# First layer: softmax denominators from blocks summed by GpSimd, once a chunk, and numerators in 32-column tiles

## What is computed

```python
kc = k.reshape(B, H, Nc, CHUNK, Dh)          # Nc = 8 chunks of 256 keys
scores = einsum('bhnd,bhjcd->bhnjc', q, kc) / sqrt(Dh)
scores = clip(scores, -10, 10)
scores = where(mask == 0, -10, scores)       # mask: adjacency
attn = softmax(scores, axis=-1)              # over the 256 keys of a chunk
ctx = einsum('bhnjc,bhjcd->bhnd', attn, vc)  # summed over the chunks
out = layernorm(ctx @ Wo.T + bo + x) * gamma + beta
```

## Time and profile before

| | |
|---|---|
| median of 3 runs | 4966.05 us (4965.57 to 4966.41) |
| the profiled execution | 4965.84 us, span 4964.0 us |
| TensorE (PE) busy | 4617.1 us, 93% |
| VectorE (DVE) busy | 3681.5 us, 74% |
| ScalarE (ACT) busy | 2924.1 us, 59% |
| GpSimd (POOL) busy | 1947.7 us, 39% |

### The profile page before, as it was taken

The page is one execution under the profiler, slowest core; times in us unless marked ns, Lnnn a source line. Parts: engine busy times, 40 slices in busy tenths (PEclk is TensorE's granted clock), DMA queues, the critical chain, the costliest instruction groups (busy, mean ns, idle before and its releaser), DMA issues. The chain is left out here.

```text
span 4964.0 us, 78134 instructions
## 1 busy us (share of the span) xinstructions
PE 4617.1 (93%) x31752; PEld 2705.9 (55%) x31752; DVE 3681.5 (74%) x5434; ACT 2924.1 (59%) x3373; POOL 1947.7 (39%) x1391
## 2 busy tenths in 40 slices
PE   5999999998999999999999899947999999999998
PEld 2334333333433433433333343327999999999998
DVE  4676677678577677667767857747889889898896
ACT  3553555455455355355445545518878888788785
POOL 1133222232232223223223323225657576666585
PEclk9999999999999999999999999968999999999999
DMA  5000000000100000000000000011112112111111
GB/s 186 1 18 9 26 9 18 26 9 9 34 9 9 19 16 18 9 26 14 13 26 9 13 14 9 9 35 49 50 47 77 30 68 76 34 65 54 47 56 44
DMA packets 126665, 160.50 MB, mean 32 GB/s; under 512 B 8545, under 2 KB 108897, under 8 KB 126305
## 3 DMA queue, kind: packets, MB, share of 16 engines
q1 hardware_dynamic: 126304, 155.49, 9.7%
HBM read 121.64 MB, written 33.83 MB: 31 GB/s over the span
## 5 line engine op out<-in xcount | busy, mean ns | idle before, releaser
L421 ACT ACTIVATE e_sb<-e_sb 128x1024 f32<-128x1024 f32 x1024 | 1080.4, 1056 | 1186.6 <-DVE e_sb L512 1171.4
L512 DVE SCALAR_TENSOR_TENSOR e_sb<-psS,mask 128x1024 f32<-128x1024 f32 x1024 | 1225.8, 1216 | 473.8 <-PE psS L628 460.1
L1229 PE MATMUL psA<-xy,ring_p 128*128 128x195 bf16 x8192 | 1399.4, 248 | 19.6 <-DVE red L1109 19.6
L1229 PE MATMUL psA<-xy,ring_s 128*128 128x195 bf16 x8192 | 1399.0, 248 | 0.0
L628 PE MATMUL psS<-qT,kT 64*128 64x512 f32 x4096 | 1089.7, 617 | 57.3 <-DVE e_sb L512 57.3
L1029 ACT ACTIVATE ring_s<-eiB,ejb 128x1024 int8<-128x1024 f32 x1024 | 1088.5, 1135 | 8.5 <-PE psA L1229 8.5
L641 PE MATMUL psN<-e_sb,v_sb 128*64 128x512 f32 x4096 | 1000.1, 609 | 0.0
L352 POOL TENSOR_TENSOR ctxT<-ctxT,num 128x512 f32<-128x512 f32 x384 | 486.3, 1275 | 1009.0 <-DVE num L492 1009.0
L1229 PEld LDWEIGHTS psA<-xy,ring_p 128*128 128x128 fp8e4 x8192 | 799.5, 98 | 24.9 <-DVE red L1109 22.5
L1229 PEld LDWEIGHTS psA<-xy,ring_s 128*128 128x128 fp8e4 x8192 | 798.7, 97 | 8.0 <-issue 0.3
L628 PEld LDWEIGHTS psS<-qT,kT 64*128 64x128 f32 x4096 | 460.2, 187 | 464.2 <-issue 234.7
(11 more groups left out here) (104 smaller groups left out, 4010.5 us busy)
## 6 DMA issues: line engine op xcount, KB each, us to landing
eiB<-ei_between SPq DMA_DIRECT2D x64, 512.0 KB, 4.2
xin<-x SPq DMA_DIRECT2D x32, 512.0 KB, 6.7
xr<-x SPq DMA_DIRECT2D x32, 512.0 KB, 3.8
x_between<-hy SPq DMA_DIRECT2D x32, 512.0 KB, 2.9
xin<-x_between SPq DMA_DIRECT2D x32, 512.0 KB, 5.6
xo<-x_between SPq DMA_DIRECT2D x32, 512.0 KB, 4.4
out<-o_sb SPq DMA_DIRECT2D x32, 512.0 KB, 5.2
e_sb<-adjT SPq DMA_DIRECT2D x4, 2048.0 KB, 9.6
```

Source lines behind the costliest of these rows:

```text
L421: act.activation(e_sb[:, s % ES], e_sb[:, s % ES], ACT.Exp, scale=SCALE).then_inc(exp_done, 1)
L512: dve.scalar_tensor_tensor(out=e_sb[:, s % ES], in0=psS[:, s % 2], scalar=-CLIP_RAW, in1=mask[:, kb, cols][:, None, :].to_broadcast([P, 2, ...
L1229: ins = pe.matmul(psA[:, i % BANKS, br * PARTS * XW:(br + 1) * PARTS * XW], part[:, n % RING, k, tt * TW + j * P:tt * TW + (j + 1) * P], x ...
```

## The change

GpSimd adds the two exponential blocks of a chunk and pair of heads into a ring of four buffers `e_sum`, at the step after the second block. TensorE takes the denominators from these, four matmuls a chunk instead of eight, four steps after the last block (`DLAG`). The numerators are written as four matmuls with 32 output columns each in place of two with 64. The ring `e_sb` has 8 buffers in place of 6, and VectorE's clip waits for the numerators and the sum of the block it overwrites instead of the denominators. The copy of the sums, the reciprocals and the split move to `ss` 3, (4, 5, 6, 6) and 7, the copy behind the exponential of its step.

```diff
 LAG = 2
-ES = 6
+DLAG = 4
+ES = 8
+SUMS = 4
-SUMS_AT, INV_AT, SPLIT_AT, PICK_AT, RES_AT = 2, 2, 6, 8, 8
+SUMS_AT, INV_AT, SPLIT_AT, PICK_AT, RES_AT = 3, (4, 5, 6, 6), 7, 8, 8
...
+            def sum_blocks(b, g):
+                n = b * (BSTEPS // KPC) + g
+                pool.wait_ge(exp_done, b * BSTEPS + KPC * (g + 1))
+                if n >= SUMS:
+                    pool.wait_ge(sums_done, (n - SUMS) // PAIRS + 1)
+                pool.tensor_tensor(e_sum[:, g % SUMS], e_sb[:, KPC * g % ES], e_sb[:, (KPC * g + 1) % ES], ALU.add)\
+                    .then_inc(esum_done, 1)
...
             def step(b, s):
+                if s % KPC == 0 and KPC <= s <= BSTEPS:
+                    sum_blocks(b, s // KPC - 1)
...
                     if s >= ES:
-                        dve.wait_ge(sums_done, b * (BSTEPS // 2) + chunk_sums_until(s - ES))
+                        dve.wait_ge(num_done, b * GROUPS + (s - ES) // KPC + 1)
+                        dve.wait_ge(esum_done, b * GROUPS + (s - ES) // KPC + 1)
...
-                if half is not None and INV_AT <= ss < INV_AT + TB:
-                    cols = slice((ss - INV_AT) * P, (ss - INV_AT + 1) * P)
-                    if ss == INV_AT:
-                        dve.wait_ge(sums_read, b * HALVES + half + 1)
-                    ins = dve.reciprocal(r_f[:, cols], r_f[:, cols])
+                for j in range(TB):
+                    if half is not None and ss == INV_AT[j]:
+                        cols = slice(j * P, (j + 1) * P)
+                        if j == 0:
+                            dve.wait_ge(sums_read, b * HALVES + half + 1)
+                        ins = dve.reciprocal(r_f[:, cols], r_f[:, cols])
...
-                for i in range(2):
-                    hd = 2 * pair + i
-                    ins = pe.matmul(psN[64 * i:64 * i + 64, pair, :], v_sb[:, kb, hd * D:(hd + 1) * D],
+                for part in range(4):
+                    i, col = part // 2, (2 * pair) * D + 32 * part
+                    ins = pe.matmul(psN[32 * part:32 * part + 32, pair, :], v_sb[:, kb, col:col + 32],
                                     e_sb[:, u % ES, i, :], start=u % KPC == 0, stop=u % KPC == KPC - 1,
...
             def denominators(b, u):
-                if not 0 <= u < BSTEPS or place(u)[1] != PAIRS - 1:
+                if not 0 <= u < BSTEPS or u % SPC != SPC - 1:
                     return
...
+                pe.wait_ge(esum_done, b * GROUPS + PAIRS * (ch + 1))
                 for hd in range(H):
-                    slot = (u - KPC * (PAIRS - 1 - hd // 2)) % ES
                     ins = pe.matmul(psD[32 * hd:32 * hd + 32, :], hot[:, c, :],
-                                    e_sb[:, slot, hd % 2, :], start=first, stop=last,
+                                    e_sum[:, (PAIRS * ch + hd // 2) % SUMS, hd % 2, :], start=c == 0, stop=c == CPH - 1,
```

More of the change, by code:

```diff
@@ L136, in layer0 @@
         e_sb = sb("e_sb", [P, ES, 2, TW])
+        e_sum = sb("e_sum", [P, SUMS, 2, TW])
         num = sb("num", [P, NS, TW])
@@ L177, in layer0 @@
         numcopy_done = sem("numcopy_done")
+        esum_done = sem("esum_done")
         sums_done = sem("sums_done")
@@ L371, in _ @@
                 for s in range(BSTEPS + (GAP if b + 1 < nb else TAIL)):
-                    if s >= HALF:
-                        step(b, s)
+                    step(b, s)
                     if b and s < TAIL - GAP:
@@ L404, in step @@
                     if g >= NS:
-                        act.wait_ge(ctx_done, b * SUMS + sums_until((g - NS) // GPH, (g - NS) % GPH))
+                        act.wait_ge(ctx_done, b * CTX + sums_until((g - NS) // GPH, (g - NS) % GPH))
                     act.activation(num[:, g % NS, :], psN[:, g % PAIRS, :], ACT.Copy).then_inc(numcopy_done, 1)
[L407 to L412, removed]
                 if half is not None and ss == SPLIT_AT:
@@ L421, in step @@
                     act.activation(e_sb[:, s % ES], e_sb[:, s % ES], ACT.Exp, scale=SCALE).then_inc(exp_done, 1)
+                if half is not None and ss == SUMS_AT:
+                    act.wait_ge(sums_done, b * (T * CH) + (half + 1) * CPH)
+                    if half >= 1:
+                        act.wait_ge(r_done, b * HALVES + half)
+                    act.activation(r_f[:, :], psD[:, :], ACT.Copy).then_inc(sums_read, 1)
                 if half is not None and half % 2 == 1 and ss == RES_AT:
@@ L647, in denominators @@
             def denominators(b, u):
[L648 removed]
+                if not 0 <= u < BSTEPS or u % SPC != SPC - 1:
                     return
[L650 to L653 removed]
+                ch = u // SPC
+                c = ch % CPH
+                if c == 0 and ch >= CPH:
+                    pe.wait_ge(sums_read, b * HALVES + ch // CPH)
+                pe.wait_ge(esum_done, b * GROUPS + PAIRS * (ch + 1))
                 for hd in range(H):
[L655 removed]
                     ins = pe.matmul(psD[32 * hd:32 * hd + 32, :], hot[:, c, :],
[L657 removed]
+                                    e_sum[:, (PAIRS * ch + hd // 2) % SUMS, hd % 2, :], start=c == 0, stop=c == CPH - 1,
                                     skip_group_check=True)
@@ L693, in step @@
                 if s > BSTEPS:
+                    denominators(b, s + 1 - DLAG)
                     project(b, s)
@@ L706, in step @@
                     broadcast(b, s + 1)
-                for of in (numerators, denominators):
-                    of(b, s - LAG)
-                    of(b, s + 1 - LAG)
+                numerators(b, s - LAG)
+                numerators(b, s + 1 - LAG)
+                denominators(b, s + 1 - DLAG)
             pe.wait_ge(ident_done, 1)
```

16 lines of the change are left out of this document (5 added, 11 removed).

## The result

The changed kernel takes 5088.26 us (median of four runs, 5082.6 to 5105.39) against 4965.81 us (4964.29 to 4966.41) of the kernel before on the same chip: ratio 1.0252, 95% interval 1.0233 to 1.0271. It is slower by 122 us. The forecast was 62 us slower, and its own case's range ended at 5055. The wide range reached to 5110, but for a rival, longer additions, that did not come about: that it holds the result is luck. The sign and the main mechanisms were right, the size was off by a factor of two.

A forecast was written before the change was run, and what follows sets the result against it. TensorE was taken to bound about half of each layer 0 batch, waiting for VectorE elsewhere. Stretch terms summed to +8.2, taken as +7.7 us a batch, 62 us in eight: 5028 us; own range 4990 to 5055, wide range 4850 to 5110.

The forecast's parts named there:

- longer additions: Rival: GpSimd is the bound, sums longer than 2.36 us or VectorE held twice in a row; 5108 us, chance 0.13.
- opening 16 steps: First 16 steps of a batch: 3 x 0.93 us saved less 1.0 of holds, -1.8 us.
- odd stretch: 16 steps finishing a tile's second half: -3.7 us from fewer denominators, +2.1 from the later split, -1.6 us.
- even with tail: 16 steps finishing a tile's first half, with layer norm: -3.7 + 2.8 + 1.0 + 1.2 + 2.4 = +3.7 us.
- last steps: Last 32 steps of a batch: -4, then the tail's waits and +2.7 for the next batch's layer-norm parts, +4.8 us.
- gap: After a batch's last steps: -0.9 us saved, 2 us lost waiting for GpSimd's queue, +1.1 us.
- What is removed: Denominators: four instead of eight matmuls save 0.93 us a chunk, 238 us at most; numerators in 32-column tiles: 0 us.
- What is moved: Later reciprocals and split: TensorE waits 1.4 us at step 8 (2.1 lost an odd stretch), 2.8 in even ones with layer norm.
- The shared access: GpSimd additions hold VectorE's two-input operations: +2.4 us per tile on the `hy` group, +1.2 on one `tmp` operation.
- the third queue: Gap: TensorE waits for the last sum behind GpSimd's in-order queue, about 2 us; the other two waits 1.5 us each.
- GpSimd that keeps up: Rival: GpSimd keeps up and holds nothing, -14.3 us a batch, 4852 us; chance 0.20.
- the cut in full: Rival: the halved denominators pay fully, 4966 - 238 = 4728 us; chance 0.05.

The follow-up runs named there:

- experiment 4: Changed kernel with each GpSimd sum cut to 64 of 512 columns, so denominators are wrong in value: 4855.2 us, ratio 0.978.
- experiment 1: Kernel before with only the numerators changed, to four tiles of 32 columns: 4930.7 us, ratio 0.9927.
- Experiment 3: Kernel before with 8 exponential buffers and all 512 GpSimd additions, unread, denominators still eight matmuls a chunk: 5134.55 us, ratio 1.0342.
- Experiment 5: Changed kernel with three unread matmuls ahead of TensorE's waits for the split (even stretches with tail) and last sums (gap): 5062.14 us, ratio 1.0194.
- experiment 2: Kernel before with only the sums' copy, reciprocals and split moved to steps 3, (4, 5, 6, 6) and 7: 5128.57 us, ratio 1.0327.
- experiment 9: Changed kernel with reciprocals at steps 4, 4, 5, 5 and the split at 6: 5105.62 us, ratio 1.0281.
- experiment 8: Kernel before with 8 exponential buffers and a 128x2048 GpSimd memset in place of each unread addition: 5038.21 us, ratio 1.0145.

## Why the forecast came out as it did

By its own terms, per batch, against the mean of batches 2 to 7 (the stretch lengths of before and after in brackets). The last two columns take out what the long additions do: the holds and queue waits in the forecast's sum, and the changed kernel less experiment 4, whose additions are short.

| term | forecast | measured | holds and queue waits, forecast | changed kernel less experiment 4 |
|---|---|---|---|---|
| opening 16 steps | -1.8 | -0.5 (36.8, 36.3) | 1.0 | 2.6 |
| first even stretch | -1.6 | -2.1 (39.1, 37.0) | 0 | 0 |
| odd stretch | -1.6 | -2.1 (39.1, 37.0) | 0 | 0 |
| even with tail, stretch 3 | +3.7 | +6.2 (46.5, 52.7) | 4.6 | 6.4 |
| odd, stretch 4 | -0.1 | -1.9 (39.1, 37.3) | 1.5 | 0.3 |
| even with tail, stretch 5 | +3.7 | +4.4 (46.5, 50.8) | 4.6 | 4.5 |
| last steps | +4.8 | +7.3 (94.5, 101.8) | 8.8 | 11.5 |
| gap | +1.1 | +5.5 (59.8, 65.3) | 2 | 5.4 |
| batch | +8.2, taken as +7.7 | +16.8 (401.3, 418.1) | 22.5 | 30.7 |

The holds and waits were put at 22.5 us a batch and cost 30.7, low clock behind them included: 8.2 a batch, 66 us in eight, which is about the 60 that the forecast is short.

**What is removed.** 2048 records of denominators, 0.97 us to the next group against the forecast's 0.93: right. The numerators' 0 was wrong with its sign (experiment 1, -34 us). That the forecast was too low in spite of this gift makes the losses that it missed larger than the difference of 60 us says.

**What is moved.** The odd stretch's wait came out as worked; that the stretch is 0.5 us shorter than forecast is the numerators' shape, 0.6 us there by experiment 1 (39.1 to 38.5). Its timeline, steps 6 to 8:

```profile
1524.13 1.99 PE L640 MATMUL psS<-qT,kT 64*128 64x512 f32 x8
...
1526.64 1.75 DVE L535 RECIPROCAL r_f<-r_f 128x128 f32<-128x128 f32 x2
1527.79 1.04 PE L669 MATMUL psD<-e_sum,hot 128*32 128x512 f32 x8
...
1529.39 0.74 DVE L541 SCALAR_TENSOR_TENSOR r_s<-r_s,lo_rows,r_f 128x512 fp32r<-128x512 f32 x1
1530.19 0.50 PE L686 MATMUL psM<-r_s,pick 64*128 64x512 f32 x1 [1.36 <-DVE r_s L541]
```

The broadcast starts 6.06 us after the scores of step 6 (forecast 6.1) and TensorE waits 1.36 (forecast 1.4). In the even stretch the statistics stand between, and the wait is 3.35 us:

```profile
1483.65 0.74 DVE L541 SCALAR_TENSOR_TENSOR r_s<-r_s,lo_rows,r_f 128x512 fp32r<-128x512 f32 x1
1484.45 0.79 PE L686 MATMUL psM<-r_s,pick 64*128 64x512 f32 x1 [3.35 <-DVE r_s L541]
1484.46 3.34 PE L640 MATMUL psS<-qT,kT 64*128 64x512 f32 x6
```

Forecast: 2.8 for the two reciprocals and the clip. The longest of these waits, 5.6 us and more, stands in the last 16 steps of each of batches 1 to 7. What the forecast didn't have is the last line: six records of scores take 3.34 us, where eight take 1.99 with the clock up. The windows from that broadcast on and ahead of it, with the granted clock as the third number from the end:

```profile
1484.45:1487.70 3.25, 3.25 (x10) 2.49 (x10) 1.48 (x4) 0.86 (x2) 2.35 (x1) 0.50 0.00 0
1480.00:1484.40 4.40, 1.09 (x12) 0.13 (x4) 4.32 (x13) 1.49 (x3) 0.75 (x1) 0.98 0.00 0
```

In the 4.4 us before it TensorE worked 1.09 us at 0.98, nearly all of it at 2.4 GHz; after it 3.25 of 3.25 us at 0.50, 1.2 GHz.

**The shared access.** The mechanism was right in each instance that I named, and in the tails the size too: VectorE is busy 3.1 and 3.0 us longer in stretches 3 and 5, where the two terms together were 3.6. The timeline of steps 11 to 14 of the same stretch, against the earlier trace rows:

```profile
1496.80 4.35 DVE L554 TENSOR_SCALAR hy<-hy,mv,rs 128x256 f32<-128x256 f32 x4
1496.96 1.37 POOL L356 TENSOR_TENSOR ctxT<-num 128x512 f32<-128x512 f32 x1 [2.15 <-DVE num L502]
1498.29 2.38 POOL L339 TENSOR_TENSOR e_sum<-e_sb 128x1024 f32<-128x1024 f32 x1
```

The four `hy` operations take 4.35 us in place of 2.33, held first by the addition, then by the sum; one alone goes up to 2433 ns where the earlier trace rows have 1372. But I counted only the holds that I could place. The groups of VectorE in the fourth batch (busy us, mean ns) show the rest, against means of 342, 151, 584 and 162 ns before:

```profile
L89 DVE TENSOR_TENSOR tmp<-tmp,var 128x4 f32<-128x4 f32 x24 | 15.6, 649 | 0.8
L88 DVE SCALAR_TENSOR_TENSOR tmp<-rs 128x4 f32<-128x4 f32 x24 | 13.2, 551 | 0.1
L554 DVE TENSOR_SCALAR hy<-hy,mv,rs 128x256 f32<-128x256 f32 x16 | 12.4, 837 | 0.0
L90 DVE SCALAR_TENSOR_TENSOR rs<-tmp,rs 128x4 f32<-128x4 f32 x24 | 8.1, 338 | 0.8
```

All the three forms of four elements a partition are hit, not one: 649, 551 and 338 ns for operations whose median is 163 or 164. In the opening 16 steps the three `tmp<-rs` of the last tile's layer norm take 4.2 us in place of 0.5, and in the last 30 steps VectorE is busy 15.3 us longer, where my terms held 6.3 (1.2, 2.4 and 2.7). Over layer 0 its busy time grew by 184 us (2242.53 to 2426.18), 23 us a batch; my terms held 14.5 us of it. Experiment 3 shows that the additions alone, without a wait of TensorE for a sum and without the moved tail, make the kernel 170 us slower, and experiment 4 that without their length the rest of the change is a gain of 109. So **the step that failed is "The shared access"**: not its kind, but the size of its terms for the layer norms outside the middle tails, +1.0 in the opening (VectorE +3.7, the stretch 2.6) and +2.7 for the next batch's layer norm in the last steps (VectorE some 9 more than the forecast there).

**The queue of GpSimd.** The wait of the third queue was forecast as "about 2" in the gap. The timeline of a gap:

```profile
1294.16 2.50 POOL L363 TENSOR_TENSOR ctxT<-ctxT,num 128x512 f32<-128x512 f32 x2
1296.61 2.36 POOL L339 TENSOR_TENSOR e_sum<-e_sb 128x1024 f32<-128x1024 f32 x1
1299.02 1.07 PE L669 MATMUL psD<-e_sum,hot 128*32 128x512 f32 x8 [3.46 <-POOL e_sum L339]
1300.02 4.49 PE L583 MATMUL psS<-hT,w_s 128*128 128x512 f32 x6
```

It is 3.46 us, and the matmuls behind it take 4.49 us for 6 records, where 8 of them took 3.70 some microseconds earlier (window 1300.02 to 1305.00: granted clock 0.66). This term, +1.1, measured +5.5, is the second that was mis-sized, and the one with the largest error. The trace of the fourth batch's gap divides it: 1.5 us more of wait, 1.8 us of low clock (eight records take 5.40 us, 3.60 before), and 1.0 us of one chunk's denominators that the delay of four steps moves from the last steps into the gap. The other two of these waits, 1.5 us each in the forecast, came as 0.6 to 0.7 us and not in each batch: in stretch 4 in four of eight (37.8 or 37.9 us in batches 1, 2 and 6, 37.0 in 3, 4, 5 and 7), in stretch 6 in five. The projection's wait of 1 us came (1.06 in the trace). The ring of 8 buffers was enough, as forecast, though the sum that a clip needs is four pairs of steps old, not five or six.

**What was missing: the clock.** Layer 0 had 334 us at 1.2 GHz, 230 more than before, in the places that I read behind waits such as the 3.35 and 3.46 us above. Experiment 5 took 121 us of that away and won 26. If all of the excess costs at the same rate, the clock is about 50 us of the 122; that is an estimate, since the filled kernel had also its three matmuls to pay for.

**The rivals.** GpSimd that keeps up (4852) was measured as a kernel of its own, 4855.2. The condition doesn't hold, and that the number does is partly luck: a batch of experiment 4 is 13.9 us shorter than before and the rival had 14.3, but the stretches without a tail won 0.5 us each by the numerators' shape, which the rival had at 0, and the tails and the gap lost 0.7 and 1.0 against it. GpSimd as the bound, with sums longer than 2.36 us, is out: 2371 ns. That the split's lateness is a cost by itself is shown for the kernel before (experiment 2). For the changed kernel it isn't: experiment 9 moved it forward and won nothing. No run has the cut in full: 4728 was not reached even with short additions.

**What stays open.** By a plain sum, -34 (shape), +164 (tail) and experiment 4's -109 leave 239 us for the halved denominators, all of the 238 that they can give. The full additions then cost 233 us in the changed kernel, where they cost 170 alone. Why they cost 63 more beside the other changes, the waits for sums among them, is not shown. The 233 us of the additions' length are placed by stretch in the table, but how they divide between holds, waits for sums and the clock was not measured; only a lower bound stands for the clock, 26 us. How much of the memset kernel's advantage is the missing read and how much its shorter time is open too.

## What to carry to other kernels

Before work goes to GpSimd, count for each of VectorE's operations with two SBUF inputs, the tiny ones above all, whether a GpSimd operation can run at that moment, and charge the whole rest of it: the average load of an engine (62% here) says nothing of it. A mean over stretches hides where the cut pays: 192 of the 512 sums, in steps clear of VectorE's layer norm and with the tail at its old steps, made 4877.3 us where the kernel with the new tile shape alone takes 4930.7; all 512 with the later tail made 5088.3. Price a change of shape between groups of matmuls from two rows of which one has the change and the other has not.

## What the runs showed of the hardware that was not expected

- A switch of the tiles' shape between two groups of matmuls has a price that the kernel's own rows can hide: 16 records of four 32-column tiles are followed by the next such group after 1.74 us, 8 records of two 64-column tiles after 1.86, while scores follow either after 1.85 and 1.87. With 0.03 us more on the way to the scores that was 34 us in 256 chunks.
- A GpSimd memset lets VectorE's operations with two inputs pass at their own 150 to 165 ns, 107 of 107, while an addition holds them until it ends (up to 2270 ns), as theory 1 of experiment 8 had it. The Trainium skill (SBUF — State Buffer, Who interferes with whom) says the same of this lock: a VectorE instruction with two SBUF inputs contends with a GpSimd one that reads SBUF, not with one that only writes it. Not expected was the operation with one tensor input and a scalar (`hy<-hy,mv,rs`): it is held by both, and in experiment 8 by two in a row (3099 ns) when the second is a memset, 16 times of 24; where the second was an addition, in experiment 3 and in the changed kernel, none of 24 waited for both (1372 ns at most).
- Idle times of TensorE of 2 us can be followed by matmuls at 1.2 GHz (3.34 us for six records of scores, 1.99 for eight at 2.4), but not each time. Read 1 us behind TensorE's waits in layer 0, the clock was low behind none of 25 waits of 1.4 us for the split, 16 of 32 of 2.08 us (experiment 2), 12 of 17 of 3.35 to 3.5 us for the split and 7 of 7 of 3.44 to 3.5 us in the gap. Filling such idle with work that nobody reads made the kernel 26 us faster.
